# A gated recurrence with a routed expert on one core: the same instructions, in other places of the engines' programs

## What is computed

```python
def _L0_attn_ref(x, Wg, bg, Wv, bv, Wd, bd, gate_W):
    gate_logits = jnp.einsum('bsd,dm->bsm', x, gate_W)
    top_vals, top_idx = jax.lax.top_k(gate_logits, TOPK)
    weights = jax.nn.softmax(top_vals, axis=-1)
    g = jnp.einsum('bsd,mde->mbse', x, Wg) + bg[:, None, None, :]
    v = jnp.einsum('bsd,mde->mbse', x, Wv) + bv[:, None, None, :]
    d = jnp.einsum('bsd,mde->mbse', x, Wd) + bd[:, None, None, :]
    x_scan = jax.nn.sigmoid(g) * jnp.tanh(v)
    a = 0.001 + 0.998 * jax.nn.sigmoid(d)
    h = _linear_scan(x_scan, a)
    comb = jnp.sum(jax.nn.one_hot(top_idx, M, dtype=x.dtype) * weights[..., None], axis=-2)
    return jnp.einsum('bsm,mbsd->bsd', comb, h)
...
def _L0_ffn_ref(x, ln_g, ln_b, bn_g, bn_b, bn_mean, bn_var, Wr, br, W_down, b_down, W_up, b_up):
    z = (x - mu) * jax.lax.rsqrt(var + EPS) * ln_g + ln_b
    z_sent = jnp.mean(z, axis=1)
    z_bn = (z_sent - bn_mean) * jax.lax.rsqrt(bn_var + EPS) * bn_g + bn_b
    probs = jax.nn.softmax(z_bn @ Wr + br, axis=-1)
    idx = jnp.argmax(probs, axis=-1)
    gate = jnp.take_along_axis(probs, idx[:, None], axis=1)[:, 0]
    h = jax.nn.relu(jnp.einsum('bsd,bdh->bsh', z, W_down[idx]) + b_down[idx][:, None, :])
    y = jnp.einsum('bsh,bhd->bsd', h, W_up[idx]) + b_up[idx][:, None, :]
    return y * gate[:, None, None]
x = x + _layernorm(_L0_attn_ref(_layernorm(x, axis=-1), ...), axis=-1)
x = x + _layernorm(_L0_ffn_ref(_layernorm(x, axis=-1), ...), axis=-1)
```

## Time and profile before

| | us |
|---|---|
| median of 3 runs | 694.19 (693.59 to 695.44) |
| the profiled execution | 692.3 |
| its span | 690.5 |
| TensorE busy | 610.8 (88% of the span) |
| VectorE busy | 586.9 (85%) |
| ScalarE busy | 460.5 (67%) |
| GpSimd busy | 100.9 (15%) |

### The profile page before, as it was taken

How to read it: one execution, slowest core, us unless ns; L and a number is a source line. 1 busy time by engine, 2 the same in 40 slices (tenths; PEclk the granted TensorE clock), 3 DMA queues, 4 the chain that set the end, 5 groups by cost and what they waited for, 6 DMA issues and landing times. The chain is left out here.

```text
span 690.5 us, 10277 instructions
## 1 busy us (share of the span) xinstructions
PE 610.8 (88%) x3259; PEld 312.7 (45%) x3259; DVE 586.9 (85%) x1096; ACT 460.5 (67%) x789; POOL 100.9 (15%) x103
## 2 busy tenths in 40 slices
PE   3799999899999999899999999899999997989432
PEld 1345454445544554445544554444544554444321
DVE  6699688998889888998889888998889888778846
ACT  3657555896579666986589666987589667657213
POOL 2002012101121102101121102101121101112101
PEclk9999999999999999999999999999999999999655
DMA  8652636162533617171724626161816433301121
GB/s 227 142 183 39 146 63 243 20 130 47 204 103 75 120 59 251 31 133 33 233 73 92 103 79 227 42 122 31 271 33 116 79 122 124 59 14 32 31 72 61
DMA packets 74905, 73.63 MB, mean 107 GB/s; under 512 B 36166, under 2 KB 66154, under 8 KB 74858
## 3 DMA queue, kind: packets, MB, share of 16 engines
q1 hardware_dynamic: 69676, 56.30, 28.8%
q0 software_dynamic: 5184, 16.78, 13.3%
HBM read 38.85 MB, written 8.52 MB: 69 GB/s over the span
## 5 line engine op out<-in xcount | busy, mean ns | idle before, releaser
L1332 PE MATMUL ps_main<-xh,w_hi 128*128 128x512 f16 x768 | 293.9, 383 | 16.0 <-ACT gate_s L574 9.3
L1332 PE MATMUL ps_main<-xh,w_lo 128*128 128x512 f16 x768 | 293.5, 382 | 0.0
L1332 PE MATMUL ps_main<-xl,w_hi 128*128 128x512 f16 x768 | 293.3, 382 | 0.0
L884 DVE TENSOR_TENSOR_SCAN hid<-decay_s,hid 128x1024 f32<-128x1024 f32 (+1 forms) x64 | 138.2, 2159 | 6.6
L574 ACT ACTIVATE decay_s<-ps_main,vecs 128x512 f32<-128x512 f32 x128 | 88.1, 688 | 72.9 <-PE ps_main L1332 72.1
L574 ACT ACTIVATE hid<-ps_main,vecs 128x512 f32<-128x512 f32 x128 | 88.3, 690 | 62.3 <-PE ps_main L1332 61.9
L1332 PEld LDWEIGHTS ps_main<-xh,w_hi 128*128 128x128 f16 x768 | 76.4, 99 | 110.1 <-ACT gate_s L574 16.1
L1332 PEld LDWEIGHTS ps_main<-xl,w_hi 128*128 128x128 f16 x768 | 75.7, 99 | 92.4 <-issue 3.0
L1332 PEld LDWEIGHTS ps_main<-xh,w_lo 128*128 128x128 f16 x768 | 75.7, 99 | 85.0 <-issue 2.3
L574 ACT ACTIVATE gate_s<-ps_main,vecs 128x512 f32<-128x512 f32 x128 | 87.7, 685 | 29.9 <-PE ps_main L1332 28.8
L896 DVE TENSOR_TENSOR hid<-hid,comb_all 128x1024 f32<-128x1024 f32 (+1 forms) x72 | 79.6, 1106 | 2.5
(11 more groups left out here) (139 smaller groups left out, 581.3 us busy)
## 6 DMA issues: line engine op xcount, KB each, us to landing
comb_all<-comb_dram SPq DMA_DIRECT2D x32, 512.0 KB, 5.5
hid<-hid POOLq DMA_DIRECT2D x28, 512.0 KB, 4.6
x_in<-in_L_attn_x SPq DMA_DIRECT2D x16, 512.0 KB, 10.0
resid<-in_L_attn_x SPq DMA_DIRECT2D x8, 1024.0 KB, 5.9
out<-resid SPq DMA_DIRECT2D x7, 1024.0 KB, 9.9
hid<-hid POOLq DMA_DIRECT2D x8, 256.0 KB, 3.3
expert<-experts SPq DMA_DIRECT2D x8, 192.5 KB, 2.2
w_stage<-in_L_attn_Wg SPq DMA_DIRECT2D x4, 256.0 KB, 3.5
```

What stands on the lines that cost most here:

```text
L884: dve.tensor_tensor_scan(states(pc), staged(decay_s, pc, pc.c), states(pc), start, ALU.mult, ALU.add).then_inc(scanned, 1)
L1332: ins = pe.matmul(ps_main[:, i % BANKS], w[:, 3 * m + kind, k, half * P:(half + 1) * P], v[:, bt.par, span(c), k], start=(n == 0), stop=(n ...
```

## The change

No instruction is added or removed. Pieces of the engines' programs change their places. ScalarE in `run_first`, in `run` (the output rows in four pairs of tiles at the readings 43 to 46) and in `last`:

```diff
         high_x(bt, 1)
-    if i == 2:
+    if i == 3:
         high_gate_weights()
-    if i == 4:
+    if i == 6:
         mixer_high(2)
-        mixer_high(3)
-    if i == 5:
+    if i == 7:
         shares(bt)
-    if i == 22:
+        mixer_high(3)
+    if i == 21:
         normalise_x(nx, tiles(0))
+    if i == 25:
         normalise_x(nx, tiles(1))
...
         high_rows_x(nx, 0)
-    if i == 27:
+    if i == 30:
         high_rows_x(nx, 1)
```

```diff
         high_u(pv, 1)
-    if i == 24:
+    if i == 23:
         normalise_x(nx, tiles(0))
+    if i == 24:
         router_sigmoids(pv)
...
         high_h(pv, 1)
-    if i == 44:
-        shares(nx)
-    if i == 45:
+    if i == 43:
         act.wait_ge(xh_moved, 16 * nx.n)
...
         act.wait_ge(y_scaled, pv.n + 1)
-        scale_rows(pv, (0, 1, 2), normed)
+        scale_rows(pv, (0, 1), normed)
+    if i == 44:
+        shares(nx)
+        scale_rows(pv, (2, 3), normed)
+    if i == 45:
+        scale_rows(pv, (4, 5), normed)
+    if i == 46:
+        scale_rows(pv, (6, 7), normed)
     evacuate(bt, i, bank, False)
-scale_rows(pv, (3, 4, 5), normed)
-scale_rows(pv, (6, 7), normed)
```

```diff
         normalise_t(pv, tiles(1))
-    if i == 14:
         high_u(pv, 0)
+    if i == 15:
         high_u(pv, 1)
-    if i == 21:
+    if i == 17:
         router_sigmoids(pv)
-    if i == 24:
+    if i == 23:
         hidden_part(pv, 0)
+    if i == 24:
         hidden_part(pv, 1)
-    if i == 26:
+    if i == 25:
         high_h(pv, 0)
-    if i == 28:
+    if i == 27:
         high_h(pv, 1)
...
         scale_rows(pv, (7,), late_rows)
-    if i == 47:
-        normalise_first_t(bt)
     evacuate(bt, i, bank, False)
+normalise_first_t(bt)
 high_u(bt, 0)
```

VectorE before the first batch, and in `run_first`, `run` and `last`, with batch 7's own second layer at the end:

```diff
             x_moments(first, 1)
-            copy_vecs()
             low_x(first, 0)
+            copy_vecs()
             low_matrix(0, VALUE)
...
 mixer_low(1)
-prepare_down(prep, 0)
 set_ones()
...
 mixer_low(2)
-copy_weights(bt, True)
 mixer_low(3)
-prepare_router(prep)
-prepare_down(prep, 1)
+copy_weights(bt, True)
 prepare_up_biases(prep)
+prepare_router(prep)
+prepare_down(prep, 0)
 multiply(bt, pcs[0])
...
 scan(bt, pcs[1])
-scale_x(nx)
 weigh(bt, pcs[1])
+scale_x(nx)
+prepare_down(prep, 1)
 multiply(bt, pcs[2])
...
 weigh(bt, pcs[2])
+prepare_hidden_biases(prep)
 multiply(bt, pcs[3])
...
 low_rows_x(nx)
-prepare_hidden_biases(prep)
 rank_mixers(nx)
...
 scan(bt, pcs[7])
-copy_weights(nx, False)
 weigh(bt, pcs[7])
+copy_weights(nx, False)
```

```diff
 t_moments(pv)
-scale_t(pv)
 x_moments(nx)
+scale_t(pv)
 multiply(bt, pcs[1])
...
 route_logits(pv)
+route_pick(pv)
 multiply(bt, pcs[3])
 scan(bt, pcs[3])
-route_pick(pv)
 weigh(bt, pcs[3])
...
 scale_y(pv)
-weights_of(nx)
 multiply(bt, pcs[6])
...
 weigh(bt, pcs[6])
+weights_of(nx)
+copy_weights(nx, False)
 multiply(bt, pcs[7])
...
 weigh(bt, pcs[7])
-copy_weights(nx, False)
 finish(pv)
```

```diff
 t_moments(pv)
-scale_t(pv)
 multiply(bt, pcs[0])
 scan(bt, pcs[0])
+scale_t(pv)
 weigh(bt, pcs[0])
...
 weigh(bt, pcs[2])
-low_u(pv)
 multiply(bt, pcs[3])
...
 weigh(bt, pcs[3])
+low_u(pv)
 route_logits(pv)
...
 weigh(bt, pcs[5])
-join_h(pv, 0)
 multiply(bt, pcs[6])
...
 weigh(bt, pcs[6])
+join_h(pv, 0)
 join_h(pv, 1)
...
 t_moments(bt, 0)
-scale_t(bt, 0)
 multiply(bt, pcs[12])
...
 weigh(bt, pcs[12])
+scale_t(bt, 0)
 multiply(bt, pcs[13])
...
 a_moments(bt, 1)
-low_u(bt, 0)
 residual(bt, 1)
...
 normalise("t", t_rows(bt), t_scaled, u_ready, bt, 1)
+low_u(bt, 0)
+low_u(bt, 1)
 route_logits(bt)
+route_pick(bt)
 finish_late(pv, None)
-low_u(bt, 1)
 join_h(bt, 0)
-route_pick(bt)
 join_h(bt, 1)
```

TensorE in the three bodies:

```diff
         turn_vecs()
-    if i == 2:
+    if i == 1:
         turn_x(bt, 1)
-    if i == 6:
+    if i == 5:
         first_gates(bt)
...
         turn_weights(bt)
-    if i == 21:
+    if i == 15:
         hidden_bias()
-    if i == 36:
+    if i == 38:
         pe.wait_ge(experts_ready, 6)
```

```diff
         turn_u(pv)
-    if i == 26:
+    if i == 23:
         route(pv)
-    if i == 29:
+    if i == 28:
         down(pv)
-    if i == 40:
+    if i == 38:
         up(pv)
+    if i == 39:
         gates(nx)
```

```diff
 for i, bank in enumerate(banks(bt)):
-    if i == 3:
+    if i == 2:
         turn_planes(pv, (4, 5, 6, 7))
-    if i == 15:
-        turn_u(pv)
     if i == 16:
+        turn_u(pv)
+    if i == 19:
         route(pv)
-    if i == 23:
+    if i == 22:
         down(pv)
...
         turn_planes(bt, TURNED, 0)
-    if i == 47:
-        turn_u(bt, 0)
     product(bt, i, bank, False)
+turn_u(bt, 0)
 pe.wait_ge(y_normed, T * (B - 1) + 1)
```

More of the change, by code:

```diff
@@ L658, in run_first @@
                         high_x(bt, 1)
-                    if i == 2:
+                    if i == 3:
                         high_gate_weights()
-                    if i == 4:
+                    if i == 6:
                         mixer_high(2)
+                    if i == 7:
+                        shares(bt)
                         mixer_high(3)
-                    if i == 5:
-                        shares(bt)
-                    if i == 22:
+                    if i == 21:
                         normalise_x(nx, tiles(0))
+                    if i == 25:
                         normalise_x(nx, tiles(1))
@@ L685, in run @@
                         high_u(pv, 1)
+                    if i == 23:
+                        normalise_x(nx, tiles(0))
                     if i == 24:
-                        normalise_x(nx, tiles(0))
                         router_sigmoids(pv)
@@ L717, in last @@
                         normalise_t(pv, tiles(1))
[L718 removed]
                         high_u(pv, 0)
+                    if i == 15:
                         high_u(pv, 1)
[L721 removed]
+                    if i == 17:
                         router_sigmoids(pv)
+                    if i == 23:
+                        hidden_part(pv, 0)
                     if i == 24:
[L724 removed]
                         hidden_part(pv, 1)
[L726 removed]
+                    if i == 25:
                         high_h(pv, 0)
[L728 removed]
+                    if i == 27:
                         high_h(pv, 1)
@@ L1018, in _ @@
             x_moments(first, 1)
+            low_x(first, 0)
             copy_vecs()
-            low_x(first, 0)
             low_matrix(0, VALUE)
@@ L1101, in run_first @@
                 mixer_low(2)
+                mixer_low(3)
                 copy_weights(bt, True)
-                mixer_low(3)
+                prepare_up_biases(prep)
                 prepare_router(prep)
-                prepare_down(prep, 1)
-                prepare_up_biases(prep)
+                prepare_down(prep, 0)
                 multiply(bt, pcs[0])
@@ L1112, in run_first @@
                 scan(bt, pcs[1])
+                weigh(bt, pcs[1])
                 scale_x(nx)
-                weigh(bt, pcs[1])
+                prepare_down(prep, 1)
                 multiply(bt, pcs[2])
@@ L1136, in run_first @@
                 scan(bt, pcs[7])
+                weigh(bt, pcs[7])
                 copy_weights(nx, False)
-                weigh(bt, pcs[7])
             def run(bt, nx, pv):
@@ L1147, in run @@
                 t_moments(pv)
+                x_moments(nx)
                 scale_t(pv)
-                x_moments(nx)
                 multiply(bt, pcs[1])
@@ L1458, in last @@
                 for i, bank in enumerate(banks(bt)):
-                    if i == 3:
+                    if i == 2:
                         turn_planes(pv, (4, 5, 6, 7))
-                    if i == 15:
+                    if i == 16:
                         turn_u(pv)
-                    if i == 16:
+                    if i == 19:
                         route(pv)
-                    if i == 23:
+                    if i == 22:
                         down(pv)
```

## The result

The changed kernel takes 807.22 us, median of 4 runs (800.92 to 815.67); the kernel before took 693.89 beside it. The ratio is 1.161 (95% interval 1.1525 to 1.170). The forecast was 682, with 676 to 689 as its range. The profiled execution took 800.92 us, 108.6 more than that of before, with a span of 799.1.

A forecast was written before the change was run, and what follows sets the result against it. TensorE's work was taken to bound a middle batch, with some 3.9 us standing still. Savings of 6.3 + 3.4 + 1.2 + 1.0 + 0.2 = 12.1 us from a median of 694.19 gave 682, range 676 to 689.

The forecast's parts named there:

- the second half of the interval: Middle batch, down product to next start: 38.43 less a 0.59 wait plus one product of 1.30, so 39.14 us.
- 75.50: Middle batches: interval from start to start, 36.36 up to the down product plus 39.14 behind it, 1.27 us less.
- the forecast of 6.3 us less: Middle batches: 1.27 us less in each of five intervals, with bounds of 3.0 to 9.5.
- 3.4 said: Last batch: the stretch up to y's statistics ends 3.4 us earlier, with bounds of 1.8 to 5.0.
- The power was put 0.9 us later: Last batch: GpSimd's power beside a multiply and scan takes 2.53 us instead of 1.64, so t's shift comes 0.9 later.
- u was put at half clock: Last batch: turning u on TensorE still takes 3.6 us; at full clock 1.6 us more would be won.
- 1.16 and 1.0 said: Tail: 1.16 us from filling the wait at t's shift of the last half, 1.0 from an earlier last down product.
- 0.2 said: First batch: moved weight copies and x's second rows win 0.2 us, between 1.5 won and 2.2 lost.
- (a): Rival, middle batches: waits come back at the router and expert's copy, only 0.6 an interval remains; 685 us, chance 0.17.
- (d): Rival, whole kernel: orders change but what is late next is as late; 692 to 696 us, chance 0.04.
- (b): Rival, last batch: GpSimd's power ends only 1.64 behind the scan, shift 1.1 later again; 683 us, chance 0.08.
- (c): Rival: TensorE's waits of 1.05, 0.5, 0.7 lower its clock; one fall 692, two 701 us; chance 0.04 each.

The follow-up runs named there:

- kept apart: The changed kernel with GpSimd's second to fourth plane additions of a middle batch waiting until both transposes of the next x have landed: 684.87 us.
- pick undone: The changed kernel with VectorE's pick of the expert put back behind the scan of piece 3, as before the change: 683.60 us.

## Why the prediction was wrong

**The step that failed** is the second half of the interval, "from the down product to the next start", put at 39.14 with "one more product" and no wait in it. TensorE's gates stand in that half, and they wait for the transposes. The prediction moved x's rows and VectorE's pieces, which release SyncE's transposes and GpSimd's additions, and never set the two issues side by side; no rival had them either. What the runs put in its place: an issue 0.40 us nearer turned transposes of 7 and 8 us into 16 and 29, 105.5 us of waits in six batches, and some 2.8 us a batch (76.02 less 73.19) at the lower clock behind them.

**The rest of the middle batch was right.** VectorE's waits at t's shift fell from 15.5 us in nine to 1.4 in two, both behind the loop (before and after, columns as in the list of waits above):

```profile
DVE shift_t L799 <- POOL root_t L464: 15.5, 9, 1.9
```

```profile
DVE shift_t L804 <- POOL root_t L464: 1.4, 2, 1.1
```

TensorE's waits are 1.04 at u (1.05 said), 0.49 at the router (0.5), 0.45 at the down product (0.7), none early in the batch but for two at turns of the loop (2.08 and 2.24), and ScalarE has none at y's shift in a middle batch. With the collision away a batch without a turn of the loop takes 75.25 us (kept apart) and 75.26 (pick undone: turned planes at 253.76 and 329.02), where 75.50 was said. The collapsed batch of the first section agrees: 96.17 less 18.16 less 2.83 is 75.2.

**The turn of the loop** was in no step. Kept apart, two of five intervals hold a turn and cost 4.4 us more each, which takes back what the short batches gave: this version isn't faster than the one with the old middle batches (684.87 and 685.46). In the profiled executions the five intervals took 383.87 us before, 385.22 kept apart, 379.97 with the pick undone and 379.49 kept apart with the weights made earlier. So the forecast of 6.3 us less, with 3.0 as its lower bound, was mis-sized, collision aside: between 1.4 us more and 4.4 less came of it.

**The last batch** came as said and larger. y's statistics: 3.4 said, 44.59 less 40.21 = 4.4 measured; t's shift waits 0.27 instead of 1.88. Two terms were off there, both to the good. The power was put 0.9 us later and came 0.3 later (1.95 us instead of 1.64; the row of 2.53 stood beside a multiply of 1024 columns, this one beside 512). And u was put at half clock, but was turned in 1.97 us behind a wait of 0.50, where before it took 3.62 behind 4.25; the prediction priced that at 1.6. Of the 2.2 us that the two make, 1.0 came through to y's statistics. The tail: 1.16 and 1.0 said, 2.65 measured; the 1.16 us wait is gone, and the last down product waits for its copy, in the changed kernel too:

```profile
778.22 3.25 PE L1387 MATMUL ps_aux<-u_split,expert 128*128 128x512 f16 x8 [4.14 <-DMA expert<-experts]
```

**The first batch**, 0.2 said: the gates begin at 78.78 us, and their wait of 1.29 is gone. The last planes of batch 0 are turned at 101.58 us in the changed kernel, 102.35 kept apart, 102.82 with the pick undone, and 102.46 before, so it lies within what executions differ by.

**The rivals.** (a) and (d) are contradicted by the waits. (b) too: in the last batch the power took 1.95 us beside the multiply and the scan and ended 0.2 us behind the scan, not 1.64. (c) named the clock and had its cause wrong: it fell behind waits of 14 to 22 us, not those of 1.05, 0.5 and 0.7, beside which it stayed at 1.00 in the versions without collision. Those versions, 683.6 to 685.4, lie in the range, so without the failed step it would have held; but in part by luck, since the last batch gave 7.0 us where 5.6 was said and made up for middle batches that gave too little.

## What to carry to other kernels

When a reordering moves what releases a DMA, set the issue times of all queues side by side and read their distance, before and after; a distance of half a microsecond between two transfers that nothing orders is a hidden condition of the old time. Where a transpose and GpSimd's accumulating transfers share a phase, order them with a wait: here it cost nothing that the runs can tell (684.87 us, against 685.42 and 683.60 without the wait), and the transposes landed in 4.6 and 5.0 us instead of 6.9 and 7.8. When an edit brings a loss far larger than anything on the list of costs, undo the edits one at a time around the resource that got slow, since one line may hold it all.

## What the runs showed of the hardware

DMA transposes from SyncE's queue and accumulating transfers from GpSimd's, each 4.6 to 5 us alone, can take 14 to 37 us beside each other, at 59 to 62 GB/s instead of 190. It depends on the start. Leads of 0.03 to 0.08 us for the transpose collapse, 0.15 to 0.18 stretches the transposes to 10 and 12 (medians) and the addition to 10, and 0.37 to 0.54 still costs some 2 to 3 us each. On the other side there is an edge: an addition 0.04 us ahead took 6.7 us, those 0.03 to 0.08 behind 14 to 18, and those 0.64 or more ahead 5.0 to 5.1. TensorE's turn of a loop cost from 0 to 2.7 us of standing still, and up to 4.4 us with the lower clock that followed; each time it stood, a packet of instructions had ended 1.7 to 1.9 us before.
